# A float32 attention core on one Trainium2 core: in one more unit, neighbouring blocks of exponentials are added on VectorE before their column sum

## The reference

```python
q, k, v = (heads(query), heads(key), heads(value))      # 16 heads of 32, float32
scores = jnp.einsum('bhqd,bhkd->bhqk', q, k)
scores = jnp.where(causal, scores, -jnp.inf)
at = jax.nn.softmax(scores / jnp.sqrt(jnp.float32(HEAD_DIM)), axis=-1)
out = jnp.einsum('bhqk,bhkd->bhqd', at, v)...
return out @ w_o + b_o
```

## Time and profile before

| | |
|---|---|
| median of three runs | 1169.7 us (1168.97 to 1173.29) |
| profiled execution, whole | 1170.05 us |
| its span | 1168.2 us |
| TensorE busy, mean granted clock | 1041.7 us, 0.981 of full |
| VectorE / ScalarE / GpSimd busy | 868.6 / 826.6 / 346.4 us |

### The profile page before, as it was taken

One profiled execution on the slowest core, in us unless ns is written; L12 is line 12 of the kernel. 1 busy time (PEld: TensorE's weight loads), 2 busy tenths in 40 slices (PEclk: granted clock), 3 DMA queues, 4 the chain that ended last, 5 costly groups with the idle time before them and its releaser, 6 DMA issues.

```text
span 1168.2 us, 17817 instructions
## 1 busy us (share of the span) xinstructions
PE 1041.7 (89%) x5799; PEld 472.6 (40%) x5830; DVE 868.6 (74%) x2207; ACT 826.6 (71%) x1260; POOL 346.4 (30%) x385
## 2 busy tenths in 40 slices
PE   0777999998899799999999799999999799998886
PEld 0333455554454333233344233232344345554443
DVE  4878899988981787885632777885535799999893
ACT  4689898898746656667616665667647988989862
POOL 1222344443552050101310131002311144434355
PEclk9998999998999999999999999999999999999998
DMA  9654525634000144210101252110043353564200
GB/s 366 181 100 83 100 56 109 109 68 101 2 1 9 47 101 82 56 38 2 36 23 26 50 111 60 46 38 2 19 90 73 73 109 77 106 127 95 51 19 36
DMA packets 34923, 84.06 MB, mean 72 GB/s; under 512 B 5749, under 2 KB 9720, under 8 KB 30841
## 3 DMA queue, kind: packets, MB, share of 16 engines
q0 software_dynamic: 12544, 47.71, 22.0%
q1 hardware_dynamic: 22266, 35.04, 9.5%
HBM read 65.81 MB, written 4.21 MB: 60 GB/s over the span
## 4 chain that ended last, share of the span: by engine, by line
PE 53%; DVE 23%; issue 8%; ACT 5%; POOL 5%; SPq 1%; DVEq 1%; DMA 0%; another core or an unknown queue 0%; POOLq 0%; ACTq 0%
PE zP L588 11%; PE oP L636 7%; PE oP L755 5%; PE zP L741 5%; PE xP L764 4%; PE hP L720 4%; DVE arena L1434 3%; DVE m L1442 3%; PE zP L683 3%; PE zP L797 2%; PE hP L797 2%; POOL ln L1109 2%; POOL ln L1102 2%; PE zP L720 2%; DVE arena L1383 2%
## 5 line engine op out<-in xcount | busy, mean ns | idle before, releaser
L919 ACT ACTIVATE arena<-arena,X 128x2048 int8<-128x2048 f32 x154 | 308.0, 2006 | 7.9 <-DVE X L1414 5.4
L985 ACT ACTIVATE arena<-zP,asc 128x512 f32<-128x512 f32 (+3 forms) x384 | 201.4, 583 | 104.4 <-PE zP L745 76.6
L588 PE MATMUL zP<-T,arena 128*128 128x512 f16 x1024 | 242.6, 386 | 0.8
L636 PE MATMUL oP<-T,arena 128*128 128x512 f16 x832 | 199.3, 383 | 1.9 <-DVE arena L1529 1.8
L588 PEld LDWEIGHTS zP<-T,arena 128*128 128x128 f16 x1024 | 102.2, 100 | 122.3 <-issue 10.9
L875 ACT ACTIVATE arena<-zP,sc 128x512 f32<-128x512 f32 x128 | 87.3, 688 | 68.7 <-PE zP L588 68.6
L636 PEld LDWEIGHTS oP<-T,arena 128*128 128x128 f16 x832 | 81.4, 99 | 81.3 <-issue 7.2
L741 PE MATMUL zP<-arena 98*128 98x512 f16 (+3 forms) x384 | 110.8, 333 | 1.6 <-ACT arena L985 1.4
L1650 DVE CUSTOM_DVE_ANT_0 scored<-hP,causal 128x128 bf16<-128x128 f32 (+3 forms) x170 | 81.0, 484 | 25.0 <-PE hP L720 23.1
L1206 POOL TENSOR_TENSOR arena<-arena 128x512 f32<-128x512 f32 x16 | 20.8, 1302 | 243.8 <-DVE arena L1680 221.6
L720 PE MATMUL hP<-arena 96*128 96x512 f16 (+3 forms) x256 | 83.1, 343 | 8.9 <-DVE mx L1650 6.2
(11 more groups left out here) (209 smaller groups left out, 1770.8 us busy)
## 6 DMA issues: line engine op xcount, KB each, us to landing
arena<-bz_row POOLq DMA_DIRECT2D x26, 1024.0 KB, 7.9
arena<-arena SPq DMA_DIRECT2D x168, 64.0 KB, 2.0
x_sb<-bet_row POOLq DMA_DIRECT2D x8, 1024.0 KB, 12.8
arena<-bz_row POOLq DMA_DIRECT2D x6, 768.0 KB, 6.4
arena<-in_w_synT SPq DMA_DIRECT2D x4, 1024.0 KB, 8.3
arena<-in_w_outT SPq DMA_DIRECT2D x4, 1024.0 KB, 15.2
x_sb<-in_b_o POOLq DMA_DIRECT2D x2, 2048.0 KB, 17.2
out_dram<-x_sb SPq DMA_DIRECT2D x16, 256.0 KB, 2.0
```

Of the source, the lines that this page charges most:

```text
L588: mm = pe.matmul(zP[:, c * CW:(c + 1) * CW], part[:, g % 2, k, :], T1[:, k, c * CW:(c + 1) * CW], start=(n == 0 and k == 0), stop=(n == 1 ...
L636: mm = pe.matmul(o, part[:, k, :], T2[:, k, :], start=(c == 0 and n == 0 and k == 0), stop=False)
L919: act.activation(junk[:, counted[0] % 2, :], Z[:, g % ZR, :], ACT.Sign, bias=X[:, 2, k:k + 1], accum_out=S[:, k:k + 1]).then_inc(sm["cnt"], 1)
L985: act.activation(PT[:, m // 4 % 2, h, q0:512], colP[m % 3][:, q0:512], ACT.Exp, scale=asc[:, g, 10:11]).then_inc(sm["exp_done"], 1)
```

## The change

`pairs` gives the long unit's three pairs to unit (2, 1) as well, so blocks 0 and 1, 2 and 3, and 4 and 5 (from column 128 on) of it are added on VectorE and summed by one matmul group each.

```diff
 def pairs(g, qc):
 
-    return () if g < GROUPS - 1 else ((0, P),) if qc == 0 else ((0, 0), (2, 0), (4, P))
+    return () if 2 * g + qc < 5 else ((0, P),) if qc == 0 else ((0, 0), (2, 0), (4, P))
```

## The result

The changed kernel takes 1183.13 us (median of five, 1179.97 to 1185.74) against 1171.19 us for the kernel before (median of five); ratio 1.0098, 95% interval 1.0084 to 1.0111. That is slower, as forecast, but by 11.9 us where 6.6 were forecast, and outside the range, which ended at 1180.5. Its profiled execution took 1185.74 us (span 1183.8), the longest of the five.

A forecast was written before the change was run, and what follows sets the result against it. TensorE was taken as the bound in unit (2,1), with VectorE's slack too small for the adds. 1170.05 + 5.0 (delay, two batches) + 1.6 (clock) = 1176.65, or 1176.3 us on the median's scale; range 1171.5 to 1180.5.

The forecast's parts named there:

- what bounds: Unit (2,1) up to the turn of the last maxima: TensorE sets the pace, busy 19.16 of 19.42 us.
- the queue: Unit (2,1), VectorE: two sets of adds, 4.68 us, ahead of row maxima with 3.7 slack; turn 2.07 us late.
- walked: Forecast by stepping through unit (2,1)'s order with trace latencies: unit end 2.5 us late per batch, 5.0 in all.
- TensorE's sums: Unit (2,1): sum matmuls net 2.81 us less per unit; behind the turn, 0.46 us more.
- Clock: TensorE's granted clock falling in unit (2,1): 1.5 to 1.6 us per fall, one fall taken, +1.6 us.
- none, one or both: Number of the two batches in which TensorE's clock falls in unit (2,1); one was taken, +1.6 us.
- Faster: Rival: adds vanish in VectorE's gaps and TensorE keeps its 5.6 us, giving 1164.1 us; chance 0.06.
- Adds stretch: Rival: both sets among unit (2,1)'s maxima take 3.92 us, 3.2 more per batch, giving 1181 us; chance 0.08.

The follow-up runs named there:

- e1_filler: Changed kernel with matmuls over zeros filling TensorE's idle time in unit (2,1): 1177.82 us, ratio 1.0061 to the kernel before.
- e2_adds_only: Changed kernel with unit (2,1)'s adds still made on VectorE, but TensorE summing every block by itself: 1175.95 us, ratio 1.0035 to the kernel before.
- e3_pair0: Changed kernel with only the pair of blocks 0 and 1 in unit (2,1): 1177.57 us, ratio 1.0058 to the kernel before.
- e5_pair2: Changed kernel with only the pair of blocks 2 and 3 in unit (2,1), on VectorE: 1177.07 us, ratio 1.0055 to the kernel before.
- e4_pair4: Changed kernel with only the pair of blocks 4 and 5 in unit (2,1), on VectorE: 1170.75 us, ratio 1.0001 to the kernel before.
- e6_pool_unit5: Changed kernel with unit (2,1)'s adds for blocks 0 to 3 moved from VectorE to GpSimd: 1170.1 us, ratio 0.9994 to the kernel before.

## Why the prediction was wrong

**Right: what bounds, and the queue.** TensorE's saving didn't matter and VectorE's queue did. L1641 has 56 records, 32 before. The wait at 526.12 is 1.28 us for 1.3 walked. With the clock held the unit is 2.74 us longer for 2.5 walked, and the turn 2.22 late for 2.07 (e1_filler); with the adds alone it is 1.92 (e2_adds_only). The changed kernel's late turn of 5.24 us (24.66 less 19.42) is thus about 2.2 of queue and 3.0 of clock in the first batch; in the second it is 3.81, 2.2 and 1.6.

**Right: TensorE's sums.** Behind the turn 8.19 us stand against 7.67 + 0.46 = 8.13 of the prediction.

**Failed: the step "Clock".** It put 1.6 us into the sum, an estimate from the 3.25 us stretch at 0.50 in the earlier trace rows. No run shows that term for the whole of the change; in the profiled execution it was 8.8 (4.59 + 4.20). Three things were off in it.

First, it looked for a fall only at the longest wait, the one before the turn, and took the stretch from 524.8 to 528, a wait of 1.28 us and row matmuls held singly at their banks, as harmless. The first fall comes right there, and e3_pair0 shows it with no longer wait. The trace of before had such a case, at the start of the core, and the step didn't use it: three waits for row maxima, none above 1.41 us, and the clock at 0.50 from about 407 to 414.

```profile
406.14 0.39 PE L720 MATMUL hP<-arena 96*128 96x512 f16 x1 [1.17 <-DVE mx L1650]
407.94 0.39 PE L720 MATMUL zP<-arena 96*128 96x256 f16 x1 [1.41 <-DVE mx L1654]
409.34 0.61 PE L720 MATMUL hP<-arena 96*128 96x512 f16 x1 [1.01 <-DVE mx L1650]
...
407.20:413.90 6.70, 4.95 (x16) 1.86 (x16) 6.56 (x19) 1.77 (x3) 4.18 (x9) 0.50 0.42 92
```

Second, it read the price from the one row of a 3.25 us stretch, while this one is twice as long. Against e1_filler, the two short falls of the changed kernel cost 1.57 and 1.59 us (behind the turn in the first batch, ahead of it in the second), as the step had it, and so do those of e3_pair0 and e5_pair2, 1.45 and 1.58. The two long ones, 528 to 535 and 804.5 to 811, cost 3.02 and 2.61.

Third, it took one fall in one batch of two, where each batch had two. The bound "none, one or both" was too narrow by that, and with it the range.

The profiled execution is the longest of the five. Taking 5.5 us from each of the five, for the queue and the sums, leaves 3.3 us in the shortest, 6.4 in the median and 9.1 in the longest, each above my 1.6; that all of it is the clock is shown for the profiled one alone. The mean granted clock of the five agrees: 0.975 in that one and 0.977 in the other four, against 0.978 to 0.983 in the 23 executions of the kernel before beside e4_pair4.

TensorE's longest wait in the unit is 2.67 us, and the clock fell four times. The stretch from 526 to 528 holds row matmuls released one at a time, but no run here parts them from the wait of 1.28 us ahead of them.

**The rivals.** "Faster" was refuted deeper than I argued. It was priced at all of TensorE's 5.6 us, but even with the early adds on GpSimd only 0.58 us per batch come (e6_pool_unit5): with TensorE relieved, it waits for the maxima and for the turn instead. "Adds stretch" didn't happen, a set took 2.40 us from its start to the next maximum's (522.97 to 525.37) for 2.34 forecast. Its 1181 came near the measured time for the wrong reason.

**Open.** Why the chip lowers the clock in one batch and not in its twin, and which of the four falls a median execution has; only one execution of each kernel was profiled, so that e1_filler and e2_adds_only show no fall in the unit rests on one trace each and on their times.

## What to carry to other kernels

Before moving work from a bound engine to one that is "only" 80% busy, look at what stands behind the new work in that engine's order and who waits for it: slack that lies ahead of the insertion, or behind a later one, can't be used. Where the engine relieved is TensorE, add up its idle and near-idle stretches in the new schedule, not just the longest wait (in e3_pair0 the clock read 0.50 in one batch behind a wait of 1.28 us, its longest), and price each with a possible fall of the clock, per repetition. And price the gain by the next engine's pace: here the trace shows a fifth of what the removed matmuls promised, at best, and the times can't tell that from none.

## What the runs showed of the hardware

TensorE's granted clock fell from 1.00 (524 to 526) to 0.50 at 528, after a wait of 1.28 us and row matmuls released one at a time (TensorE busy 0.84 us of 524 to 526 and 1.61 of 526 to 528), and stayed there while TensorE was busy all the time (530 to 534, clock 0.50). In the kernel before it fell at about 407, among waits of 1.17, 1.41 and 1.01 us, to 0.50 (407.2 to 413.9). After a wait of 2.75 us (e5_pair2) it fell in one batch (0.50 in 538 to 540) and held in the other (1.00 in 800 to 802). The same sequence of matmuls and waits, run twice in one execution, lost the clock once and kept it once (e3_pair0: 22.78 us at a mean clock of 0.93 against 21.33 at 1.00; e5_pair2: 10.35 at 0.84 against 8.77 at 1.00). With matmuls over zeros in TensorE's idle time, which do nothing for the result, the clock stayed at 1.00 and the kernel took 5.3 us less (1177.82 for 1183.13, e1_filler). GpSimd's float32 adds of 128 x 512, 1.24 us each (4.96 for four), ran beside VectorE's maxima without lengthening them (mean to the turn 0.689 us a maximum of 512 columns, 0.687 before).
